# The sixteen denominators of an attention layer raised to the power -1 on GpSimd, and VectorE's division moved behind the next low half

## What is computed

```
def step(carry, qkv):
    K_sum, KV = carry
    q_t, k_t, v_t = qkv
    K_sum = K_sum + k_t
    KV = KV + k_t[..., :, None] * v_t[..., None, :]
    num = jnp.einsum('bhd,bhde->bhe', q_t, KV)
    den = jnp.maximum(jnp.einsum('bhd,bhd->bh', q_t, K_sum), EPS)
    return ((K_sum, KV), num / den[..., None])
...
x = x + _L0_attn_ref(xn, L0_attn_Wq, L0_attn_Wk, L0_attn_Wv, L0_attn_Wo) + _L0_ffn_ref(xn, L0_ffn_Wg, L0_ffn_bg, L0_ffn_W1, L0_ffn_b1, L0_ffn_W2, L0_ffn_b2)
...
x = x + _L1_attn_ref(xn, L1_attn_w_qkv, L1_attn_w_proj, L1_attn_b_proj) + _L1_ffn_ref(xn, L1_ffn_W_r, L1_ffn_W_k, L1_ffn_W_v, L1_ffn_mu_r, L1_ffn_mu_k)
```

## Time and profile before

| | us |
|---|---|
| median of 3 runs | 383.14 |
| lowest and highest run | 381.67, 383.59 |
| the profiled execution | 381.57 |
| its span | 379.5 |

### The profile page before, as it was taken

How to read it: one execution, slowest core, us unless ns; L and a number is a source line. 1 busy time by engine, 2 the same in 40 slices (tenths; PEclk the granted TensorE clock), 3 DMA queues, 4 the chain that set the end, 5 groups by cost and what they waited for, 6 DMA issues and landing times. The chain is left out here.

```text
span 379.5 us, 9047 instructions
## 1 busy us (share of the span) xinstructions
PE 339.8 (90%) x2425; PEld 297.1 (78%) x2425; DVE 320.4 (84%) x590; ACT 281.0 (74%) x821; POOL 222.4 (59%) x239
## 2 busy tenths in 40 slices
PE   8999599999999997999897989898159899999996
PEld 3887244989999986889897989898149678887885
DVE  5999989899999996897998889986505799999665
ACT  3988946878999885888785869697036887776861
POOL 3898005838766886566676677678740238883210
PEclk9999979999999999999999999999668999999999
DMA  6882991544454543546454645565220002120001
GB/s 171 235 226 60 351 343 48 149 128 138 134 150 141 150 148 105 167 133 175 140 153 136 156 137 159 135 169 139 55 70 28 16 1 58 55 58 28 28 29 55
DMA packets 47120, 47.02 MB, mean 124 GB/s; under 512 B 8529, under 2 KB 35313, under 8 KB 46817
## 3 DMA queue, kind: packets, MB, share of 16 engines
q1 hardware_dynamic: 42032, 37.23, 32.2%
q0 software_dynamic: 4320, 8.86, 9.6%
q10 hardware_dynamic: 720, 0.38, 0.4%
HBM read 32.88 MB, written 13.50 MB: 122 GB/s over the span
## 5 line engine op out<-in xcount | busy, mean ns | idle before, releaser
L503 POOL DMA_INDIRECT xg<-xn_rows,slot_tok x71 | 81.5, 1148 | 58.4 <-DVE slot_at L1815 23.4
L604 ACT ACTIVATE xT<-banks,b1T 128x128 f32<-128x128 f32 x284 | 82.0, 381 | 24.9 <-remote 12.9
L520 POOL DMA_INDIRECT qk_exp<-expert_rows,ranki x64 | 70.7, 1104 | 18.5 <-issue 18.3
L587 PE MATMUL banks<-w_sb,xT 128*128 x568 | 77.2, 279 | 1.2 <-issue 1.1
L575 PE MATMUL banks<-xgT,w 128*128 128x128 f32 x568 | 77.7, 281 | 0.1
L587 PEld LDWEIGHTS banks<-w_sb,xT 128*128 128x128 f32 x568 | 70.8, 195 | 1.1 <-issue 0.3
L575 PEld LDWEIGHTS banks<-xgT,w 128*128 128x128 f32 x568 | 70.6, 195 | 0.6 <-issue 0.5
L790 DVE TENSOR_TENSOR cq<-banks,phi 128x1152 f32<-128x1152 f32 x32 | 43.2, 1351 | 15.7 <-remote 9.3
L703 DVE TENSOR_TENSOR low<-outer,high 128x1152 fp32r<-128x1152 f32 (+1 forms) x32 | 39.2, 1225 | 20.2 <-ACT high L696 16.4
L801 DVE TENSOR_REDUCE late<-cq 128x144 f32<-128x1152 f32 (+1 forms) x32 | 45.5, 1422 | 0.1
L696 ACT CAST high<-outer 128x1152 fp32r<-128x1152 f32 x32 | 36.9, 1154 | 7.7 <-DVE outer L685 4.0
(11 more groups left out here) (224 smaller groups left out, 717.5 us busy)
## 6 DMA issues: line engine op xcount, KB each, us to landing
w<-in_L_ffn_W SPq DMA_DIRECT2D x71, 256.0 KB
expert_rows<-ye SPq DMA_DIRECT2D x71, 64.0 KB
expert_rows<-x_sb SPq DMA_DIRECT2D x2, 2048.0 KB, 10.4
x_sb<-in_L_attn_x SPq DMA_DIRECT2D x8, 256.0 KB, 4.2
xn_rows<-xn_all SPq DMA_DIRECT2D x8, 256.0 KB, 2.9
w_sb<-in_L_ffn_W SPq DMA_DIRECT2D x8, 256.0 KB, 4.2
out<-outer SPq DMA_DIRECT2D x7, 256.0 KB, 2.4
xg<-xn_rows,slot_tok POOLq DMA_INDIRECT x71
```

Source lines behind the costliest of these rows:

```text
L503: pool.indirect_dma_start(out=xg[n][:, :], out_offset=None, in_=xn_dram, in_offset=bass.IndirectOffsetOnAxis(ap=slot_tok[:, j:j + 1], axis ...
L520: pool.indirect_dma_start(out=y_moe[:, i, k, :], out_offset=None, in_=y_dram, in_offset=bass.IndirectOffsetOnAxis(ap=ranki[:, 0, k, i:i + ...
L587: last = nc.tensor.matmul(y, hidT[p][:, c, :], w2_sb[:, ds(e * NC + c, 1), :], start=(c == 0), stop=(c == NC - 1))
L604: last = nc.scalar.activation(hidT[p][:, c, :], slot_bank(j)[:, c * P:(c + 1) * P], ACT.Gelu_apprx_tanh, bias=b1T[:, ds(e * NC + c, 1)])
```

## The change

`attn_reciprocal` becomes an instruction of GpSimd: a tensor_tensor with the operation pow on the same 128 x 32 denominators and a new 128 x 16 tile `all_minus` of -1.0 that is read twice. It waits for `sums_ready` as the old one did and raises the same semaphore `rden_ready`. It stands in GpSimd's list at the 16 slots at which the sum of an r = 1 tile runs (`SUMS_AT[1:NT:2]`), behind that slot's gather and low third and ahead of that slot's gathers of results. On VectorE the reciprocal goes and `attn_divide` moves behind `attn_low`. One more memset at GpSimd's start fills `all_minus`; the counts of `pool_const` go up by one.

```diff
--- before.py
+++ after.py
@@ -131,6 +131,7 @@
     mv = [sbuf(f"mv{p}", [P, GT, 2]) for p in range(NG)]
     ve = [sbuf(f"ve{p}", [P, GT]) for p in range(NG)]
     minus = [sbuf(f"minus{p}", [P, GT]) for p in range(NG)]
+    all_minus = sbuf("all_minus", [P, H])
     mhalf, eps4, zero4 = (sbuf(name, [P, GT]) for name in ("mhalf", "eps4", "zero4"))
     rstd = [sbuf(f"rstd{p}", [P, GT]) for p in range(NG)]
     shift = [sbuf(f"shift{p}", [P, GT]) for p in range(NG)]
@@ -738,7 +739,7 @@
             b = KV_AT.index(j)
             pe.wait_ge(phi_ready, b + 1)
             if b == 0:
-                pe.wait_ge(pool_const, 5)
+                pe.wait_ge(pool_const, 6)
             nc.tensor.matmul(bank[:, 4 * D - DA:4 * D], phib[b % 2][:, 0, D:2 * D], qkv3[:, 2 * b, 2 * D:2 * D + DA],
                              start=True, stop=True)
         if j in QT_AT:
@@ -802,9 +803,10 @@
                                 ).then_inc(sums_ready, 1)
 
 
-    def attn_reciprocal(v, b):
-        v.wait_ge(sums_ready, 2 * b + 2)
-        nc.vector.reciprocal(rden, sums[:, :, :, DH]).then_inc(rden_ready, 1)
+    def attn_reciprocal(pool, b):
+        pool.wait_ge(sums_ready, 2 * b + 2)
+        nc.gpsimd.tensor_tensor(rden, sums[:, :, :, DH], all_minus[:, :].unsqueeze(1).broadcast_to([P, 2, H]), ALU.pow
+                                ).then_inc(rden_ready, 1)
 
     def attn_divide(v, b):
 
@@ -1522,7 +1524,7 @@
                     nc.scalar.activation(scrap["scalar"], scrap["zero"], ACT.Exp)
 
             def first():
-                act.wait_ge(pool_const, 4)
+                act.wait_ge(pool_const, 5)
                 nc.scalar.activation(scrap["scalar"], scrap["zero"], ACT.Gelu_apprx_tanh).then_inc(warmed, 1)
                 attn_tokens(act, 0)
                 attn_keys(act, 0, 0, 0)
@@ -1542,9 +1544,9 @@
 
         @block.gpsimd
         def _(pool):
-            for a, x in ((mhalf[:, :], -0.5), (eps4[:, :], EPS_LN), (zero4[:, :], 0.0), (scrap["zero"], 0.0)):
+            for a, x in ((mhalf[:, :], -0.5), (eps4[:, :], EPS_LN), (zero4[:, :], 0.0), (scrap["zero"], 0.0), (all_minus[:, :], -1.0)):
                 nc.gpsimd.memset(a, x).then_inc(pool_const, 1)
-            pool.wait_ge(pool_const, 4)
+            pool.wait_ge(pool_const, 5)
             for g in range(5):
                 deviation(pool, 0, g, g)
             for g in range(NG):
@@ -1567,6 +1569,8 @@
                     gather(pool, j + AHEAD)
                 if j in SUMS_AT[0:LOW_SHARED]:
                     attn_low_third(pool, SUMS_AT.index(j) + 1)
+                if j in SUMS_AT[1:NT:2]:
+                    attn_reciprocal(pool, SUMS_AT.index(j) // 2)
                 for q, at in enumerate(Y_AT):
                     if j == at:
                         gathers_y(pool, q, 1)
@@ -1857,11 +1861,10 @@
                 if r == 1 and till(b, B - 2):
                     attn_mask_KV(v, b + 1)
                 attn_sums(v, i, r)
-                if r == 1:
-                    attn_reciprocal(v, b)
-                    attn_divide(v, b)
                 if till(b, B - 2):
                     attn_low(v, b + 1, r, 1 - p)
+                if r == 1:
+                    attn_divide(v, b)
                 if r == 1 and till(b, B - 3):
                     phi(v, b + 2, p)
             for b in range(2):
```

## The result

The changed kernel takes 468.99 us, median of 6 runs (460.68 to 470.08), where the kernel before takes 382.40 us (380.08 to 385.09): 1.217 times as long, 95% interval 1.207 to 1.227. The forecast was 463 us with a range of 387 to 480, so sign and size hold, and so does the main cause, a power on GpSimd that costs by the column. The four terms of its sum hold less well: the second stretch is 14.3 us too small, the third has the wrong sign, and the first is right because two errors cancel. The profiled execution took 467.41 us, its span 465.3 us.

A forecast was written before the change was run, and what follows sets the result against it. VectorE was taken to bound the first stretch alone and share the second with TensorE, something else the third; 25.6 + 42.5 + 6.4 + 6.4 = 80.9 us on 381.57 gave 462.5, stated as 463 us, range 387 to 480.

The forecast's parts named there:

- four terms: Added times of three windows and the end of the kernel: 25.6 + 42.5 + 6.4 + 6.4 = 80.9 us.
- second stretch: Nine sequences, 127.62 us before: 6.4 us more VectorE chain each, its 15.1 us of old waits absorbed, +42.5 us.
- first stretch: Four sequences, 44.15 us before, VectorE full: each grows by 6.4 us, +25.6 us.
- The price of the power: New 128 x 32 power on GpSimd: 1.07 to 6.68 us, upper end taken, 0.2025 us for each column.
- Rivals 1 and 2: Power on GpSimd at a fixed price, 388 us, chance 0.14; or partly fixed, 400 to 442 us, chance 0.25.
- Low half and power take turns, whoever comes first: VectorE's low half and GpSimd's power exclude each other, so the low half, 0.95 to 1.35 us, is no cover.
- The rival that the change hides what it means to hide: Power starts ahead of VectorE's low half and is short: about 380 us, chance 0.05.
- The price of a sequence, d: Growth of VectorE's chain per sequence: 6.68 + 0.10 - 0.42 = 6.36 us, called 6.4.
- Third stretch: Two sequences, 39.90 us before: the first power counts, the second falls into an existing VectorE wait, +6.4 us.
- Rival 3: Powers break GpSimd's run of 13 DMAs near the last gathers, ending the standstill: worth 19.2 us, chance 0.06.
- The last sequence: End of the kernel: no low half behind the power, the combining of expert results waits, +6.4 us.

The follow-up runs named there:

- the one try at the clock: Changed kernel plus 40 small matmuls on zeros ahead of each sequence's transposes but the first: 474.66 us, ratio 1.249 against the kernel before.
- those with two waits: Kernel before plus only the last two of GpSimd's 16 waits for the sums, in the last run of gathers: 347.94 us, ratio 1.002.
- the pacing: Kernel before, with GpSimd's last gathers of results waiting for TensorE's down product of the slot before: 347.35 us, ratio 0.999.

## Why the prediction was right, and where it was not

**What bounds the kernel before.** VectorE full in the first stretch, shared in the second: the table above bears it out for the first stretch. VectorE could absorb nothing there: its waits for the power, 17.6 us in this window, and its longer outer products, 5.0 us, both come through to the time.

**The price of the power.** Forecast 6.68 us, the upper end, out of 1.07 to 6.68. Measured 5.48. It is linear in the columns, as taken (the plain instruction of the earlier trace rows beside it, L307, is a multiplication and no addition or subtraction; at 32 columns a multiplication takes 0.26 us, and (0.26 - 0.20) / 28 gives the same 2.1 ns a column); the constant part is 0.37 us, not 0.20, so a column is (1.01 - 0.37) / 4 = 0.16 us and not 0.2025. The start-up that the prediction named as possible and gave nothing is there, and it makes the term 1.2 us too large. Rivals 1 and 2 (388 us, and 400 to 442) fall with it.

**Low half and power take turns, whoever comes first.** This step was right for one order and wrong for the other. When the low half starts first, the power waits for it: 6.57 us at 272.39, and the multiplication's 0.26 becomes 1.31. When the power starts first, as in 10 of the 15 sequences that have a low half there, the low half is not held up: 0.96 us beside a 5.48 us power. I had generalised from a low half that took 1.47 us beside a low third; why a low third holds it up and a power does not, no run here shows. The rule of the Trainium skill (SBUF — State Buffer, Who interferes with whom), by which such a pair excludes each other for a whole instruction, has the trace with it in the first order and against it in the second: by it the low half at 101.47 could not have ended before 106.45, and it ended at 102.43. The rival that the change hides what it means to hide is thus partly true: the low half does lie beside the power, but 0.96 to 1.36 us are little against 5.48.

**The price of a sequence, d.** Forecast 6.4 us. Measured from the rows of the sequence at 99.40: the sums end at 100.90, the division starts at 106.49, 5.59 us later. From the start of the sums to phi, behind low half and division in both kernels, are 106.84 - 99.40 = 7.44 us, before 95.39 - 92.26 = 3.13: 4.3 us. In a sequence whose low half comes first it is about 5.0.

**First stretch.** Forecast 25.6, measured 25.6 us, and that is two errors that cancel. d is 4.3 and 5.0 in place of 6.4, and what fills it up was not in my sum. The sequence from 99.40 to 116.36 grew by 16.96 - 10.96 = 6.0 us: 4.3 from d, 1.26 from the outer product beside the displaced low third, and 0.4 from a wait for TensorE. The one from 81.45 to 99.40, whose low half came first, grew by 17.95 - 10.93 = 7.0 us with the same outer product in it. The four together make the 25.6. The prediction asked what is queued behind the power on GpSimd and answered with the gathers and their six slots; the low third, two places further on, was the one with a neighbour that it disturbs.

**Second stretch.** Forecast 42.5, measured 56.8 us: the term that was too small. With d at about 4 (3.9 where the low half is 1.36 us long), VectorE's chain gives only 9 x 4 = 36 us, before any old wait is taken off. VectorE is idle for 184.43 - 110.01 = 74.4 us of it. Its waits in this window account for them; the last two rows are those of the kernel before in its own window:

```profile
DVE late L817 <- POOL rden L808: 38.0, 9, 5.4
DVE cq L791 <- remote: 18.4, 4, 6.3
DVE low L704 <- issue: 7.6, 8, 1.4
...
DVE low L703 <- issue: 3.4, 1, 3.4
DVE cq L790 <- remote: 3.3, 3, 1.6
```

The power brings 38.0 us, less 2.5 us that VectorE works less: the 36 of the chain. The unnamed waits go from 6.7 to 26.0 us, 19.3 more. The rest is small: the waits for ScalarE's high half stay (5.9 us before, 5.6 now), those for TensorE grow from 1.7 to 4.7 us. The assumption that failed is that the 15 us of old waits fall into the new ones. They were not absorbed, they grew, and the surplus over the chain is nearly all in the unnamed ones. They are there too with a wait of the gather queue alone (1.019) and with the multiplication (1.042), with VectorE's chain hardly longer. What makes them stays open. The granted clock of 0.85 can act on VectorE directly only through the 4.7 us; whether it has a part in the unnamed waits, the one try at the clock did not single out. The upper end of the range had this case in it, but summed it wrongly: 16 x 6.4 = 102 us on top of 381.57 are 484 and not 480.

**Third stretch.** Forecast +6.4, measured -3.4 us. The standstill of the earlier trace rows, with TensorE's gaps of 9.47 and 4.26 us, is not in this place in the changed kernel; its longest unnamed gap on TensorE among the experts is this:

```profile
244.62 0.30 PE L560 MATMUL banks<-cst,xg 128*128 128x128 f32 x1 [2.24 <-issue]
```

Rival 3 was right for the place, by 10 us, and wrong for the whole. That it is the powers' places in the run of gathers that removed it was not shown: the runs meant to test it fell on the chip that has no standstill. And VectorE stands elsewhere, for as long as at 268.30 us before:

```profile
265.86 0.94 POOL L504 DMA_INDIRECT xg<-xn_rows,slot_tok  x1 [0.30 <-issue]
...
268.19 1.36 DVE L791 TENSOR_TENSOR cq<-banks,phi 128x1152 f32<-128x1152 f32 x1 [6.33 <-remote]
```

The last of a run of DMAs without a gap ends at 266.80, VectorE is back at 268.19 after 6.33 us.

**The last sequence.** Forecast +6.4, measured +6.7 us. The sums, the power, the division and the combining behind it:

```profile
372.12 1.51 DVE L802 TENSOR_REDUCE late<-cq 128x144 f32<-128x1296 f32 x1
...
373.71 5.47 POOL L808 TENSOR_TENSOR rden<-late,all_minus 128x32 f32<-128x32 f32 x1 [4.23 <-DVE late L802]
...
379.21 0.43 DVE L817 SCALAR_TENSOR_TENSOR late<-rden,late 128x256 f32<-128x256 f32 x1 [5.59 <-POOL rden L808]
...
379.55 2.19 DVE L948 SCALAR_TENSOR_TENSOR x_sb<-qk_exp,sel,x_sb 128x128 f32<-128x128 f32 x8
```

Nothing hid the reciprocal there before, and nothing hides the power now: the wait of 5.59 us less the 0.42 saved is 5.2 us. The remaining 1.5 us lie behind the combining and were not traced to a cause; the clock of that stretch is 0.95 where it was 1.00.

**The ladder.** Where the unnamed waits exist (the kernel before at 380 to 385 us), the ratios stand in this order: the division moved, alone, 1.009; GpSimd's waits alone, 1.019; both with a multiplication in the power's place, 1.042; a power of 16 columns, 1.130; the change, 1.217 and 1.228. Of its 0.217 the length of the power, with all that it sets off, makes 1.217 - 1.042 = 0.175, or 67 us: this is shown, since nothing but the operation differs. The other 0.042, or 16 us, can be divided only roughly, for the parts were measured on different chips with intervals of about 0.01: the wait in the gathers' queue 0.019, the move 0.009, and 0.014 for the handovers and for what the parts do to one another. None of the kernels is faster than the kernel before; those with two waits and with the pacing tie with it on a chip where there was nothing to gain.

## What to carry to other kernels

Ask what an operation costs on the engine that it moves to before asking what it would hide behind: 0.35 us on VectorE for 32 columns became 5.48 us on GpSimd, and the cover was 0.96 to 1.36. Where the only row at hand is of a small shape, and the same shape has a cheaper operation beside it, the difference between the two scales with the columns until shown otherwise. A wait put into a queue that also issues DMAs can cost twice (here 0.6% and 1.9% with no work behind it): once for who needs the result, and once for everything that then leaves the queue in a lump or late, the work of a third party included.

## What the runs showed of the hardware that was not expected

- **A power on GpSimd is 0.37 us and 0.16 us a column of 128 partitions** (1.01, 2.94 and 5.48 us for 4, 16 and 32 columns), a multiplication of 4 and of 32 columns 0.20 and 0.26 us, or 0.0021 us a column. The Trainium skill (GPSIMD Engine Reference, 3.1 Elementwise) gives one figure for tensor_tensor, about 2.6 cycles an element; these runs show that it does not hold for a power, whose price by the column is some 75 times that of the multiplication.
- **Which of VectorE and GpSimd is held up when they meet goes by the pair and the order.** Behind a low half the power and the multiplication wait until it ends (6.57 for 5.48, 1.31 for 0.26 us); a low half begun during a power runs at full speed (0.96 us, or 1.36 to 1.39 for the wider ones that otherwise take 1.36; 10 of 10). A low half begun 0.39 us behind a low third is held up (1.47 for 0.95). And an outer product begun 0.38 us ahead of a low third takes 2.48 us for 1.22, four times out of four, while the low third keeps its 1.00: here the one that started first is held up, for 0.26 us more than the other lasts. (A fifth, at 149.02 us, that is 0.78 us old when the low third begins, takes its 1.22, and the low third 1.29.) Why, no run shows.
- **Unnamed waits depend on the chip.** In every trace but the four of one chip VectorE, ScalarE and TensorE stand at places with no releaser that the profile names, for up to 9 us, and once each for 13 and 19. Of VectorE's 42 "remote" waits of 1.5 us and more, 31 end 0.5 to 1.4 us behind the last of six or more indirect DMAs that GpSimd issues 0.95 us each with 0.30 between. On that one chip VectorE has none of them, the clock is 1.00 in the middle, and the kernel before takes 347.63 us in place of 380 to 385. That the run of DMAs is the cause is argued from these ends alone; against it, two waits of the kernel before end in the middle of a run (268.30 and 273.29), and on the one chip a run of 49 brings none. What it is that the engines wait for, and what the change would cost on that chip, is open.
